# Attention stage of a fused four-layer graph network: one-hots made two half-steps ahead in four buffers, and TensorE's loop unrolled by four half-steps with five registers each

## The reference, cut to what matters

```python
h = (x @ W).reshape(n, 4, 32)
a_src = (h * att_src).sum(-1)          # n x 4
a_dst = (h * att_dst).sum(-1)          # n x 4
alpha = a_src[src] + a_dst[dst]        # one row of 4 for each edge: two gathers
alpha = leaky_relu(alpha, 0.2)
# softmax over the edges of a destination, weighted sum of h[src], normalizations
```

## Time and profile before

| | us |
|---|---|
| median of 3 runs (5745.56 to 5755.92) | 5755.3 |
| the profiled execution's own time | 5750.34 |
| its span, first to last instruction | 5748.5 |
| PE busy in the span | 4340.3 |
| POOL busy | 3890.9 |
| DVE busy | 3626.2 |
| ACT busy | 1734.3 |

### The profile page before, as it was taken

The page is one execution under the profiler, slowest core; times in us unless marked ns, Lnnn a source line. Parts: engine busy times, 40 slices in busy tenths (PEclk is TensorE's granted clock), DMA queues, the critical chain, the costliest instruction groups (busy, mean ns, idle before and its releaser), DMA issues.

```text
span 5748.5 us, 124694 instructions
## 1 busy us (share of the span) xinstructions
PE 4340.3 (76%) x26535; PEld 3551.3 (62%) x26536; DVE 3626.2 (63%) x10847; ACT 1734.3 (30%) x5601; POOL 3890.9 (68%) x3352
## 2 busy tenths in 40 slices
PE   3666549999729898989577777777773688888884
PEld 3555549999719888888455555555552455555553
DVE  5666775555665444444655555555554688888886
ACT  0000000000001111111266665666663244445442
POOL 4777787770016777777288888888885477777771
PEclk6555555555555555555699888889886899999997
DMA  5666535552123233223044444444444344445441
GB/s 122 193 188 188 163 105 164 163 164 75 46 75 84 78 77 77 78 76 77 20 35 36 35 35 36 35 35 36 35 36 79 107 135 134 134 134 135 133 134 40
DMA packets 396077, 536.69 MB, mean 93 GB/s; under 512 B 86434, under 2 KB 273900, under 8 KB 396001
## 3 DMA queue, kind: packets, MB, share of 16 engines
q0 software_dynamic: 213152, 301.19, 27.6%
q1 hardware_dynamic: 134897, 125.62, 7.2%
q10 hardware_dynamic: 47952, 109.14, 6.4%
HBM read 408.63 MB, written 127.00 MB: 93 GB/s over the span
## 4 chain that ended last, share of the span: by engine, by line
PE 25%; POOL 19%; issue 17%; DMA 17%; DVE 17%; ACT 3%; SPq 1%; DVEq 1%; ACTq 1%; POOLq 0%
POOL ACCB L460 12%; DMA acc_dram<-GR,ARENA 12%; PE WIDE L613 9%; POOL acc_dram L469 5%; DMA ARENA<-p_dram,SRCI 4%; PE WIDE L615 3%; DVE ACCB L1002 3%; POOL ARENA L486 2%; DVE ARENA L1184 2%; PE WIDE L724 2%; PE WIDE L549 2%; DVE ARENA L1002 2%; PE WIDE L706 2%; DVE T L1002 2%; DVE ARENA L1522 1%
## 5 line engine op out<-in xcount | busy, mean ns | idle before, releaser
L469 POOL DMA_INDIRECT acc_dram<-GR,ARENA x830 | 1283.2, 1546 | 349.1 <-ACT GR L812 221.7
L452 POOL DMA_INDIRECT GR<-h_dram,SRCI x830 | 911.9, 1099 | 327.4 <-issue 241.6
L486 POOL DMA_INDIRECT ARENA<-p_dram,SRCI x830 | 864.5, 1042 | 302.3 <-issue 154.8
L460 POOL DMA_INDIRECT ACCB<-h_dram,SRCI x830 | 805.1, 970 | 276.6 <-issue 251.7
L724 PEld LDWEIGHTS WIDE<-ACCB 128*128 128x128 f32 x3320 | 544.4, 221 | 390.5 <-issue 283.2
L724 PE MATMUL WIDE<-ACCB 128*128 128x128 f32 x3320 | 597.0, 310 | 234.9 <-issue 234.9
L651 PE MATMUL WIDE<-ACCB 128*128 128x128 f32 x1660 | 648.4, 494 | 122.7 <-DMA ACCB<-h_dram,SRCI 84.4
L1002 DVE TENSOR_TENSOR ACCB<-iota,DLC 128x640 f32<-128x640 f32 x332 | 274.7, 827 | 695.2 <-PE WIDE L653 377.9
L1431 DVE SCALAR_TENSOR_TENSOR ACCB<-WIDE,ARENA,ACCB 128x128 f32<-128x128 f32 x1660 | 567.7, 350 | 181.3 <-ACT ACCB L910 162.5
L613 PE MATMUL WIDE<-ACCB 128*128 128x128 f32 x1660 | 642.9, 491 | 33.6 <-DVE ACCB L1002 33.6
L1006 DVE TENSOR_SCALAR ACCB<-ACCB,SRC 128x128 f32<-128x128 f16 x832 | 291.1, 350 | 480.1 <-ACT ACCB L812 472.0
(11 more groups left out here) (317 smaller groups left out, 8046.5 us busy)
## 6 DMA issues: line engine op xcount, KB each, us to landing
T<-pairs_dram ACTq DMA_DIRECT2D x167, 320.0 KB, 3.8
g_dram<-GR SPq DMA_DIRECT2D x166, 320.0 KB
ACCB<-g_dram ACTq DMA_DIRECT2D x166, 320.0 KB, 3.0
ARENA<-src_rows_dram SPq DMA_DIRECT2D x166, 160.0 KB, 3.0
GR<-h_dram,SRCI POOLq DMA_INDIRECT x830
ACCB<-h_dram,SRCI POOLq DMA_INDIRECT x830, 2.5
acc_dram<-GR,ARENA POOLq DMA_INDIRECT x830
GR<-in_attr SPq DMA_DIRECT2D x830, 16.0 KB
```

Of the source, the lines that this page charges most:

```text
L452: pool.indirect_dma_start(GR[:, q, :], None, h_dram[:, :], row_of(j)).then_inc(landed[q], 16)
L460: pool.indirect_dma_start(GX[:, q, :], None, h_dram[:, :], row_of(j)).then_inc(l1_landed[q], 16)
L469: pool.indirect_dma_start(acc_dram[q % NACC][:, :], bass.IndirectOffsetOnAxis(ap=SCI[:, j:j + 1], axis=0), GR[:, q, :], None, compute_op=A ...
L486: pool.indirect_dma_start(HC3[:, j % RING3, :], None, p_dram[:, :], bass.IndirectOffsetOnAxis(ap=SRCI[:, j:j + 1], axis=0)).then_inc(lande ...
```

## The change

The buffers of the one-hots go from two to four, VectorE makes the one-hots of half-step m+2 ahead of the picking of m, and TensorE's loop takes the form of `by_groups`, with a read of five registers ahead of each half-step.

```diff
-        OTB = carve(spread, 4 * HALF * P, 2, HALF * 2 * P)
-        OTP = carve(spread, 4 * HALF * P, 2, HALF, 2, P)
-        HIA = carve(spread, 8 * HALF * P, 2, HALF, NT)
+        OTB = carve(spread, 0, ABUFS, HALF * 2 * P)
+        OTP = carve(spread, 0, ABUFS, HALF, 2, P)
+        HIA = carve(spread, 8 * HALF * P, ABUFS, HALF, NT)
...
-            with pe.Fori(0, ITER) as i:
-                ts = tile_registers(ENG.PE, i)
-                for h in range(2):
-                    n = i * 2 + h + 1
-                    pe.wait_ge(ev("a_onehot"), n + ABUFS)
-                    pe.wait_ge(ev("a_picked"), n)
-                    pe.wait_ge(ev("a_adas_copied"), n)
-                    for k in range(HALF):
...
+            def a_values(i, g):
+
+                ts = tile_registers(ENG.PE, i, g * GROUP, LRING, GROUP)
+                h, n = g % 2, i * LONG + g + 1
+                pe.wait_ge(ev("a_onehot"), n + ABUFS)
+                pe.wait_ge(ev("a_picked"), n)
+                pe.wait_ge(ev("a_adas_copied"), n)
+                for k in range(HALF):
...
+            by_groups(pe, a_values)
...
             def a_onehot(i, b):
 
-                h = b % 2
+                m = i * ABUFS + b
                 v.wait_ge(ev(f"a_rows_landed{b}"), i * 16 + 16)
-                v.wait_ge(ev("a_picked"), i * ABUFS + b + 1)
-                ts1(OTB[:, h, :], BCAST[:, b, :], pcol[:, 0:1], ALU.is_equal)
+                if not isinstance(i, int) or m >= 2:
+                    v.wait_ge(ev("a_picked"), m - 1)
+                ts1(OTB[:, b, :], BCAST[:, b, :], pcol[:, 0:1], ALU.is_equal)
...
             def a_pick(i, b):
 
                 h, n = b % 2, i * ABUFS + b
                 v.wait_ge(ev("a_values"), n + 1)
+                v.wait_ge(ev("a_picked"), n + 2)
...
-            a_onehot(0, 0)
+            for b in range(2):
+                a_onehot(0, b)
             with v.Fori(0, GROUPS // ABUFS) as i:
                 for b in range(ABUFS):
-                    a_onehot(i + (b + 1) // ABUFS, (b + 1) % ABUFS)
+                    a_onehot(i + (b + 2) // ABUFS, (b + 2) % ABUFS)
                     a_pick(i, b)
-            a_onehot(GROUPS // ABUFS, 1)
-            a_pick(GROUPS // ABUFS, 0)
-            v.wait_ge(ev("a_picked"), 2 * ITER + 1)
-            a_pick(GROUPS // ABUFS, 1)
+            for b in range(2):
+                a_pick(GROUPS // ABUFS, b)
```

More of the change, by code:

```diff
@@ L539, in _ @@
             pe.wait_ge(ev("slots_loaded"), 32)
-            with pe.Fori(0, ITER) as i:
-                ts = tile_registers(ENG.PE, i)
-                for h in range(2):
-                    n = i * 2 + h + 1
-                    pe.wait_ge(ev("a_onehot"), n + ABUFS)
-                    pe.wait_ge(ev("a_picked"), n)
-                    pe.wait_ge(ev("a_adas_copied"), n)
-                    for k in range(HALF):
[L548 to L555, removed]
+            def a_values(i, g):
[5 more added lines that the diff above has]
+                for k in range(HALF):
+                    for part in range(3):
+                        pe.matmul(bank(h)[:, k * NT * HEADS:(k + 1) * NT * HEADS], OTP[:, g, k, 1, :],
+                                  ADNB[:, part, :, HEADS:2 * HEADS], start=(part == 0), stop=(part == 2))
+                    for part in range(3):
+                        last = pe.matmul(bank(2 + h)[:, k * 8:(k + 1) * 8], OTP[:, g, k, 0, :],
+                                         ADNB[:, part, bass.ds(ts[k], 1), :].rearrange("p a b -> p (a b)"),
+                                         start=(part == 0), stop=(part == 2))
+                last.then_inc(ev("a_values"), 1)
+            by_groups(pe, a_values)
             pe.wait_ge(stage_done, STAGE["edge_values"])
@@ L1167, in a_onehot @@
             def a_onehot(i, b):
-                h = b % 2
+                m = i * ABUFS + b
                 v.wait_ge(ev(f"a_rows_landed{b}"), i * 16 + 16)
-                v.wait_ge(ev("a_picked"), i * ABUFS + b + 1)
-                ts1(OTB[:, h, :], BCAST[:, b, :], pcol[:, 0:1], ALU.is_equal)
-                tt(HIA[:, h, :, :], iotab[:, 0:NT].unsqueeze(1).broadcast_to([P, HALF, NT]),
-                   HIC[:, bass.ds((i * ABUFS + b) * HALF, HALF)].unsqueeze(2).broadcast_to([P, HALF, NT]),
+                if not isinstance(i, int) or m >= 2:
+                    v.wait_ge(ev("a_picked"), m - 1)
+                ts1(OTB[:, b, :], BCAST[:, b, :], pcol[:, 0:1], ALU.is_equal)
+                tt(HIA[:, b, :, :], iotab[:, 0:NT].unsqueeze(1).broadcast_to([P, HALF, NT]),
+                   HIC[:, bass.ds(m * HALF, HALF)].unsqueeze(2).broadcast_to([P, HALF, NT]),
                    ALU.is_equal).then_inc(ev("a_onehot"), 1)
@@ L1180, in a_pick @@
                 v.wait_ge(ev("a_values"), n + 1)
+                v.wait_ge(ev("a_picked"), n + 2)
                 tt(PICK, bank(h)[:, 0:HALF * NT * HEADS].rearrange("p (k t c) -> p k t c", k=HALF, c=HEADS),
-                   HIA[:, h, :, :].unsqueeze(3).broadcast_to([P, HALF, NT, HEADS]), ALU.mult).then_inc(ev("a_masked"), 1)
+                   HIA[:, b, :, :].unsqueeze(3).broadcast_to([P, HALF, NT, HEADS]), ALU.mult).then_inc(ev("a_masked"), 1)
                 v.wait_ge(ev("a_masked"), n + 1)
```

## The result

The changed kernel takes 5792.6 us (median of 4 runs, 5790.0 to 5798.2) where the kernel before takes 5755.6 (4 runs): ratio 1.0070, 95% interval 1.0058 to 1.0082. It is slower by 37 us. The forecast was 5790, and the range 5768 to 5818.

What follows compares the result with a forecast made beforehand. TensorE's instruction stream was taken as the bound of the attention stage, its reads exposed. Reads 196 - 157 us, around them -4, one-hots 0: +35 on 5755.3 gives 5790 us, range 5768 to 5818.

Steps and rivals of the forecast that it cites:

- The bound: Attention stage: TensorE's instruction stream sets the pace in every half-step, 3.53 us each, and VectorE has about 1 us to spare.
- The reason that reads are exposed: TensorE's stream, with 15 address computations a half-step, hands over matmuls as the engine is ready and never gets ahead.
- One-hots two ahead, 0: VectorE's part: making one-hots two half-steps ahead with four buffers is worth 0, since PE doesn't wait there.
- Reads: TensorE's register reads in the stage: 82 of ten cost 157 us before, 165 of five cost 196 us after.
- Around the reads: Idle time at TensorE's loop ends and between half-steps, without reads: 76 us before, 72 after, 4 us less.
- Position in the table: TensorE's reads of five: short (0.597 us) at a multiple of 16 bytes, long (1.234 us) elsewhere, one short to three long.
- VectorE's waits on the changed line: VectorE's waits on PE's line 552 grow by about 35 us in the changed kernel's trace.
- Hidden reads (1): The longer body hides TensorE's reads and DVE's 2.55 us becomes the bound: 163 us less, 5592 us; 2%.
- Short reads everywhere (2): TensorE's reads of five take the short price at every position: 109 us, 48 less, total 5703 us; 3%.
- real waits on DVE (3): PE's weight loads really wait on DVE: 96.4 us go, some 61 net of dearer reads, 5694 us; 3%.
- cost by register count (4): A read costs by its registers, two of five equalling one of ten: -4, 5751 us, no change; 5%.
- The whole price of a loop's end at each inner read (5): Each inner read in TensorE's loop brings a loop end's whole price: +35 + 52, 5842 us; 6%.

Runs made afterwards that it cites:

- TensorE's part alone: Kernel before with only TensorE's loop changed to five-register reads a half-step, VectorE keeping two buffers and one-hots one ahead: 5780.8 us, ratio 1.0067.
- the reads' edits: Changed kernel with TensorE's register reads regrouped or begun elsewhere: 5740.5 us (ten registers twice a pass), 5727.3 (from multiples of 16 bytes), 5635.9 (twenty once a pass).
- the run with 5: Changed kernel with all reads kept but 5 address computations a half-step in place of 15, so some values are not the reference's: 5585.5 us, ratio 0.9719.
- The old reads in the new loop: Changed kernel, its loop of four half-steps reading ten registers twice a pass as the kernel before did: 5740.5 us, ratio 0.9995.
- the reads begun at one: Changed kernel with each read begun at the multiple of 16 bytes at or below its five numbers: 5727.3 us, ratio 0.9971.
- the reads of 6, 7, 8 and 20: Changed kernel with reads of 5, 6, 7 and 8 registers from multiples of 16 bytes, 5727.3 us; or with one read of twenty a pass, 5635.9 us.

## Why the prediction was right

- **The bound.** TensorE's instruction stream, no wait on DVE: shown by TensorE's part alone giving the whole +37, and by the reads' edits moving the time from +37 to -108 with VectorE's part unchanged.
- **The reason that reads are exposed.** 15 address computations a half-step: shown by the run with 5, in which 130 us of reads lie beside weight loads instead of 0.1. The words "as the engine is ready for it" were too kind to the engine. The stream is the slower of the two, 2.03 us a batch against 1.64.
- **One-hots two ahead, 0.** Right here, to within some 10 us, and only here: 29 us once the reads are cheap.
- **Reads.** Forecast 157 to 196 us, +39; measured 151.6 to 189.4, +37.8. Both sums were some 4% high: the mean read of ten was 1.85 us and not 1.92, in part because the idle time that was divided holds small pauses inside the batches. The 10% put on clean reads was 6% before and 7% after, and the error nearly cancels in the difference. That it does so to 1 us is luck. The old reads in the new loop took 8 us more than in the old one, at the same count and form, so reads can shift by as much with their timing alone, and the forecast had no term for it.
- **Around the reads.** Forecast -4, measured -3.6.
- **Position in the table.** The multiple of 16 bytes was right, shown by the reads begun at one. The rate that I then put on it, 0.098 us a register, was wrong, and the reads of 6, 7, 8 and 20 showed it.
- **VectorE's waits on the changed line.** Forecast +35 us, measured 137.0 to 192.3, +55. DVE's busy time fell by 8 us (403 to 396) though its instructions' durations sum to the same 423 us, so they overlap more; and the old list had 12.2 us of its waits under "issue", the new one 1.2. The two make up the difference but for 1 us.
- **Rivals.** Hidden reads (1) don't come from a longer body; a lead of the stream comes from fewer computations. Short reads everywhere (2), real waits on DVE (3), and cost by register count (4) each have a run against them. The whole price of a loop's end at each inner read (5) is refuted by 0.35 to 0.40 us there against 0.74.

## What to carry to other kernels

Where no engine is full and waits are put down to an engine that had been done long before, look at the instruction stream of the engine that starts late. In this kernel reads of tables into registers, address arithmetic and waits are work there, and they hide only while the stream is ahead of its engine. Read registers seldom, many at a time and from a multiple of 16 bytes, and count the address computations between matmuls as matmul time. A deeper prefetch of operands is worth nothing before that, and can be worth something after it: try it again when the bound has moved.

## What the runs showed of the hardware that was not expected

- A read of a table into registers goes by its start and its remainder more than by its count: eight numbers from a multiple of 16 bytes in 0.60 us, seven in 1.07, ten in 1.09, ten from elsewhere in 2.40.
- Address computations set the price of a read. With 5 of them a half-step, 0.79 of 1.18 us of each read lay beside the 1.64 us batch; with 15 it was 0.1 of 189 us over the whole stage.
- The first weight load comes 0.33 us behind the end of a read on which TensorE waits, 82 times out of 82 in the kernel before.
- Reads of one form lie up to 1 us apart in one stage (2.40 to 3.45 us for ten from byte 40, with the old reads in the new loop), and an edit that moves them in time changed their mean by 0.2 to 0.3 us (2.58 to 2.80, 1.11 to 1.37). The cause is not known.
